# Attention scores of groups 3 to 7 from fp16 halves of the normalised input, in a cross-attention and feed-forward kernel

## What is computed

```python
Q = layernorm(x) @ Wq + bq;  K = ctx @ Wk + bk;  V = ctx @ Wv + bv
scores = where(mask, Q @ K.T / sqrt(512), -1e9)
x = x + softmax(scores) @ V @ Wo + bo
h = layernorm(x)
real = h @ cos(theta + theta_noise);  imag = h @ sin(phi + phi_noise)
out = x + sqrt(real**2 + imag**2)
```

## Time and profile before

| | us |
|---|---|
| median of 3 runs (244.76 to 245.19) | 244.77 |
| the profiled execution | 245.31 |
| its span | 243.20 |
| PE busy | 235.8 (97%) |
| DVE busy | 169.6 (70%) |
| ACT busy | 145.9 (60%) |
| POOL busy | 54.4 (22%) |

### The profile page before, as it was taken

One profiled execution on the slowest core, in us unless ns is written; L12 is line 12 of the kernel. 1 busy time (PEld: TensorE's weight loads), 2 busy tenths in 40 slices (PEclk: granted clock), 3 DMA queues, 4 the chain that ended last, 5 costly groups with the idle time before them and its releaser, 6 DMA issues.

```text
span 243.2 us, 3947 instructions
## 1 busy us (share of the span) xinstructions
PE 235.8 (97%) x1260; PEld 136.6 (56%) x1260; DVE 169.6 (70%) x341; ACT 145.9 (60%) x252; POOL 54.4 (22%) x154
## 2 busy tenths in 40 slices
PE   6999999999999999999999999999999999999993
PEld 2899437457544584458544854476447744444472
DVE  1676899976897876777768775877587753873443
ACT  2222787981669347943795379546873589266442
POOL 1002175410601233023302330132104310132000
PEclk9999999999999999999999999999999999999999
DMA  6999988695258724972397258734774324413622
GB/s 192 367 428 388 377 290 158 133 352 86 46 146 210 299 82 92 255 281 93 85 252 264 108 108 237 229 160 89 232 239 175 72 57 89 172 43 86 214 92 86
DMA packets 49533, 44.80 MB, mean 184 GB/s; under 512 B 42630, under 2 KB 42886, under 8 KB 46445
## 3 DMA queue, kind: packets, MB, share of 16 engines
q1 hardware_dynamic: 48565, 43.37, 57.7%
q0 software_dynamic: 288, 1.05, 2.4%
q10 hardware_dynamic: 664, 0.18, 0.3%
HBM read 25.66 MB, written 8.39 MB: 140 GB/s over the span
## 4 chain that ended last, share of the span: by engine, by line
PE 86%; DMA 7%; SPq 3%; ACT 2%; DVE 1%; issue 0%; DVEq 0%; ACTq 0%
PE re L503 9%; PE im L503 9%; PE im L504 9%; PE re L504 9%; PE re L505 9%; PE im L505 9%; PE score_bank L551 7%; DMA angle_n<-in_theta_noise 7%; PE att L481 3%; PE att L479 2%; PE re L564 2%; PE im L564 2%; PE re L566 2%; PE im L566 2%; PE re L568 2%; PE im L568 2%
## 5 line engine op out<-in xcount | busy, mean ns | idle before, releaser
L773 ACT ACTIVATE h<-x,shift,rstd 128x512 f32<-128x512 f32 x28 | 22.7, 811 | 34.6 <-POOL shift L382 34.6
L551 PEld LDWEIGHTS score_bank<-a_keys,xTb 128*128 128x128 f32 x192 | 35.9, 190 | 8.2
L503 PE MATMUL re<-w_hi,hT 128*128 128x512 f16 x100 | 37.9, 379 | 0.0
L503 PE MATMUL im<-w_hi,hT 128*128 128x512 f16 x100 | 37.9, 379 | 0.0
L505 PE MATMUL re<-w_hi,hT 128*128 128x512 f16 x100 | 37.9, 379 | 0.0
L505 PE MATMUL im<-w_hi,hT 128*128 128x512 f16 x100 | 37.9, 379 | 0.0
L504 PE MATMUL re<-w_lo,hT 128*128 128x512 f16 x100 | 37.9, 379 | 0.0
L504 PE MATMUL im<-w_lo,hT 128*128 128x512 f16 x100 | 37.9, 379 | 0.0
L1055 DVE SCALAR_TENSOR_TENSOR h_split<-h,h_split 128x512 f16<-128x512 f32 x32 | 22.1, 692 | 20.9 <-ACT h_split L777 20.2
L551 PE MATMUL score_bank<-a_keys,xTb 128*128 128x77 f32 x192 | 32.8, 252 | 0.0
L792 ACT ACTIVATE sq_re<-re 128x512 f32<-128x512 f32 x27 | 15.8, 586 | 17.2 <-PE re L505 12.1
(11 more groups left out here) (181 smaller groups left out, 425.7 us busy)
## 6 DMA issues: line engine op xcount, KB each, us to landing
xTb<-in_xT SPq DMA_DIRECT2D x8, 1024.0 KB, 5.2
xb<-in_x SPq DMA_DIRECT2D x7, 1024.0 KB, 5.5
out_rows<-wv SPq DMA_DIRECT2D x7, 1024.0 KB, 3.9
wk<-in_Wk SPq DMA_DIRECT2D x2, 512.0 KB, 5.5
wqT<-in_WqT SPq DMA_DIRECT2D x4, 256.0 KB, 7.8
wv<-in_Wv SPq DMA_DIRECT2D x1, 1024.0 KB, 13.6
wo<-in_Wo SPq DMA_DIRECT2D x1, 1024.0 KB, 16.1
xb<-in_x SPq DMA_DIRECT2D x4, 256.0 KB, 16.2
```

Of the source, the lines that this page charges most:

```text
L503: nc.tensor.matmul(bank_[:, :], hT[j][:, 0, k, :], w_hi[part][:, k, :], start=(k == 0), stop=False)
L551: last = nc.tensor.matmul(score_bank[:, KEYS * j:KEYS * j + KEYS], xTb[:, k, P * j:P * j + P], a_keys[:, k, KEYS * batch:KEYS * batch + KEYS],
L773: nc.scalar.activation(h[j % 2][:, :], x2[b][:, j, :], ACT.Identity, bias=shift2[:, j:j + 1], scale=rstd2[:, j:j + 1]).then_inc(h_made, 1)
```

## The change

Groups 3 to 7 no longer use `xTb`. Their scores are computed from the normalised x, `y`, in fp16 halves, as the feed products are. Per group: DVE takes the statistics (`stats_of_later_x`), POOL makes `y` in four fp32 tiles (in the place of `wo`, which is free by then), ACT makes the high half (`high_of_x`) and DVE the low half (`low_of_x`), SP turns both with a DMA transpose into `yT` (in the place of `angle_n`), four per group. `a_keys` is scaled by a norm and split once into `a_split`. A score is then two matmuls: the high half of y by both halves of the keys (154 columns) and the low half by the high half of the keys (77 columns, added to the first 77). The two halves of the sum lie side by side in `score_bank` and `pT_bank`, and `logits_of_halves` adds them in four operations. The load of x comes one step earlier, in three buffers in turn, and `load_xT` goes for these groups. On PE the scores move from `feed(n,2,1)` and `feed(n,3,0)` to `feed(n,3,0)` and `feed(n,3,1)`, the last two of the step.

```diff
 # POOL
+            def normal_of_x(m):
+                rstd_of_x(m)
+                pool.wait_ge(rstd1_made, m + 1)
+                if m > SPLIT:
+                    pool.wait_ge(y_lo_made, TILES * (m - SPLIT))
...
+                for j in range(TILES):
+                    nc.gpsimd.tensor_scalar(y[j], x_of[m][:, j, :], mv1[:, j, 0:1], rstd1[:, j:j + 1],
+                                            ALU.subtract, ALU.mult).then_inc(y_made, 1)
             def step(m):
-                rstd_of_x(m + 1)
+                if m < LAST:
+                    normal_of_x(m + 1)
                 for j in range(TILES):
                     rstd_of_x2(m, j)
 # PE
+            def score_halves(m, batch, i):
...
+                if k == 0:
+                    pe.wait_ge(yT_ready[j], 16 * (m - SPLIT + 1))
+                bank_ = (score_bank, pT_bank)[j // 2]
+                at = KK * (j % 2)
+                nc.tensor.matmul(bank_[:, at:at + KK], yT[j][:, 0, k, :], a_split[:, BATCH * k + batch, :, :],
+                                 start=(k == 0), stop=False)
+                last = nc.tensor.matmul(bank_[:, at:at + KEYS], yT[j][:, 1, k, :], a_split[:, BATCH * k + batch, 0, :],
+                                        start=False, stop=(k == CH - 1))
...
+            pe.wait_ge(a_squared, 1)
+            nc.tensor.matmul(pT_bank[:, 0:1], ones_all[:, :], a_part[:, :], start=True, stop=True).then_inc(a_norm_mm, 1)
 # ACT, step(n)
                 square(n, 0, 1)
+                if more:
+                    high_of_x(n + 2, 0)
                 roots(n - 1)
+                if more:
+                    high_of_x(n + 2, 1)
                 square(n, 1, 0)
+                if more:
+                    high_of_x(n + 2, 2)
+                    high_of_x(n + 2, 3)
 # DVE, step(n)
                     softmax_shift(m, a)
+                    if more:
+                        stats_of_later_x(n + 2)
                     low_probs(m)
                     softmax_total(m)
...
-                if blk is not None:
-                    stats_of_x(b, blk)
-                    dve.wait_ge(stats1_made, m + 2)
+                if more:
+                    low_of_x(n + 2, 0)
                 finish(n - 1, a)
+                if more:
+                    low_of_x(n + 2, 1)
                 residual(m, a, 0)
+                if more:
+                    low_of_x(n + 2, 2)
                 stats_of_x2(m, a, 0)
...
```

More of the change, by code:

```diff
@@ L61 @@
 V_SCALE = 8192.0
+A_SCALE = 8192.0
+SPLIT = 3
 WARM = 11
@@ L161, in build @@
         result = wv
+        x_of = [xb[0], xb[1], xb[0], wqT, xb[1], xb[0], wqT, xb[1]]
+        y = [wo[:, j, :] for j in range(TILES)]
+        y_halves = angle_n[0][:, :].bitcast(F16)
+        y_turned = angle_n[1][:, :].bitcast(F16)
+        y_split = [y_halves[:, 2 * DIM * j:2 * DIM * j + 2 * DIM].rearrange("p (s d) -> p s d", s=2) for j in range(TILES)]
+        yT = [y_turned[:, 2 * DIM * j:2 * DIM * j + 2 * DIM].rearrange("p (s c r) -> p s c r", s=2, c=CH) for j in range(TILES)]
+        a_squares = angle_w[0][:, 0:CH * KK]
+        a_pairs = a_keys[:, :, :].rearrange("p c (b k) -> p (c b) k", b=BATCH)
         re_bank = [bank("re0"), bank("re1")]
@@ L322, in _ @@
             transpose_h(1, [1])
-            with sp.Fori(0, 2) as i:
-                step(2 * i + 1, 1, i + 1, True)
-                step(2 * i + 2, 0, i + 2, True)
-            step(5, 1, 3, True)
-            step(6, 0, 4, False)
-            step(7, 1, 4, False)
+            load_later_x(SPLIT)
+            for n in range(1, GROUPS):
+                step(n)
             for j in range(TILES - 1):
@@ L599, in step @@
                 attend(n + 1, batch, 1)
[L600 to L603 removed]
+                feed(n, 2, 1)
                 attend(n + 1, batch, 2)
                 if more:
[L606 removed]
+                    feed_and_score(n, 3, 0, n + 2, 1 - batch, 0)
                 else:
@@ L609, in step @@
                 attend(n + 1, batch, 3)
-                feed(n, 3, 1)
+                if more:
+                    feed_and_score(n, 3, 1, n + 2, 1 - batch, 2 * CH)
+                else:
+                    feed(n, 3, 1)
             pe.wait_ge(a_ready, CH)
@@ L880, in step @@
                 high_half(n + 1, 1 - b, 2)
-            step(1, 1)
-            step(2, 0)
-            with act.Fori(0, 2) as i:
-                step(2 * i + 3, 1)
-                step(2 * i + 4, 0)
+            for n in range(1, LAST):
+                step(n, n % BATCH)
             square(LAST - 1, 3, 1)
@@ L1209, in step @@
                 mean_of_x2(m, 3)
-            step(1, 1, 1)
-            step(2, 0, 2)
-            step(3, 1, 2)
-            step(4, 0, 3)
-            step(5, 1, 3)
-            step(6, 0, None)
+            for n in range(1, LAST):
+                step(n, n % BATCH)
             add_squares(LAST - 1, 3)
```

155 lines of the change are left out of this document (120 added, 35 removed).

## The result

| | before | after |
|---|---|---|
| median, us | 244.76 (244.73 to 245.19, 4 runs) | 264.97 (264.71 to 265.8, 4 runs) |
| the profiled execution | 245.31 | 264.71 |
| its span | 243.20 | 262.9 |

The changed kernel takes 1.083 times as long, with a 95% interval of 1.080 to 1.085: 20.2 us more. The forecast was 257.1, with a range of 247 to 267; the narrower range that it gave its own mechanism, 254 to 261, doesn't hold the time.

The account below looks back on a forecast made before the run. TensorE bounds the kernel before; after the change an in-order chain of VectorE, ScalarE and GpSimd does. Step 1 +4.7, steps 2 to 5 +6.5, step 6 +1.1 give +12.3: 257.6 us profiled, 257.1 median, range 247 to 267.

Parts of the forecast that it names:

- The loop: In-order chain over VectorE, ScalarE and GpSimd, from root to root: 26.94 us a step against 25.32 before.
- Rival C: The loop holds, but GpSimd slips in before the low passes: 25.13 us a step, 247.5 us; chance 0.12.
- Rival D: GpSimd's pass takes 1.6 us or more and stops VectorE: 29 us a step, 267 us; chance 0.15.
- the forecast's own range: Range for the forecast's own mechanism, the loop: 254 to 261 us around 257.1; chance 0.53.
- GpSimd's first normalised tile 0.88: Link of the loop before ScalarE's high half; a 128x512 GpSimd pass priced 0.84, ends 0.62 and 1.6 us.
- the first root: ScalarE's root in step 1, put at 84.3, 2.72 us after GpSimd's first pass at 81.5.
- TensorE's pair: Two fp16 score matmuls replacing a 0.18 us fp32 one: 0.10 us, a gain of 1.25 us a step.
- the gain vanishes into idle time: TensorE's gain, 6.2 us over five steps, lost to new idle time before attend tile 2 and at step starts.
- The waits behind low pass 3 and low half 1: GpSimd's small operations wait for VectorE operations with two SBUF inputs: 0.80 and 0.69 us on the loop.
- Rival B: TensorE stays the limit, VectorE's and ScalarE's chain fitting 24.1 us a step: 239.6 us as median; chance 0.10.
- The queue on SP: Store behind the fourth transpose, next group's first transpose behind it: 0.6 us; 3.3 us from low half to landing.

Follow-up runs that it names:

- no_y_chain: Changed kernel without the normalised tiles of groups 3 to 7, their halves and transposes; scores take transposed h as weights: 243.6 us, ratio 0.990 to the kernel before.
- port_order: Changed kernel with VectorE's low pass 3 moved behind residual 1 and tile 0's low half behind residual 2: 262.4 us, ratio 1.066 to the kernel before.
- raw_halves_2: raw_halves with one change on SP's queue, tile 0's transpose sent ahead of the store: 240.8 us, ratio 0.983 to the kernel before.
- raw_halves: Changed kernel with halves of raw x, no y tiles, three 77-column matmuls per score and a new ScalarE and VectorE order: 244.2 us, 0.995 of the kernel before.
- root_first: Changed kernel with ScalarE's high half of normalised tile 0 moved behind the root: 263.8 us, ratio 1.072 to the kernel before.
- reordered: Changed kernel with all its work, in another order on ScalarE and VectorE, and the store ahead of the y transposes: 262.3 us, ratio 1.066 to the kernel before.

## Why the prediction was right, and where it was off

**The loop was right, station by station, up to GpSimd's first pass.** The range was wide enough for the time because it took in rivals C and D; the forecast's own range was missed by 4 us. Counted from the root at 142.09, the forecast's stations and the trace's:

| station | forecast | measured |
|---|---|---|
| GpSimd's second small operation of tile 0 (L428, 150.19) | 8.10 | 8.10 |
| low half of tile 0 through (next start, 153.44) | 11.41 | 11.35 |
| logits (159.70) | 17.64 | 17.61 |
| GpSimd's first pass gets in (168.36 less 2.07) | 24.22 | 24.20 |
| high half of x (168.36) | 25.10 | 26.27 |
| next root (170.30) | 26.94 | 28.21 |

**The step that failed** is "GpSimd's first normalised tile 0.88", with its bounds of 0.62 and 1.6: 2.07 measured. The forecast scaled a 128x128 operation (0.28) by columns and took an operation without length (0.10) as the fixed part. The pass's own slope is 3.3 ns a column for two arithmetic steps, with 0.36 fixed. The upper bound, two steps for twice the price, had the right idea and a slope that was too low. The pass makes 1.17 of the 1.27 by which a turn is longer; the other 0.10 lies between the high half and the root. The four turns make 5.1 us, and the first root, forecast for 84.3, starts at 85.66, of which the pass is 1.2. Together that is 6.5 of the 7.1 us by which the profiled execution, 264.71, exceeds the forecast's 257.6. The rest isn't assigned.

**TensorE's pair**: 0.10 forecast, 0.10 measured. The Trainium skill has 81 ns for load-and-matmul pairs of 128 columns ("TensorE: Matmul & The Clock Gate", Back-to-back issue gap); by the estimate from it the pair would take 0.16. That doesn't show here: the 77-column matmuls pass at 0.036 each between long ones. That the gain vanishes into idle time was right, and no_y_chain shows it is there to be had.

**The waits behind low pass 3 and low half 1** (0.80 and 0.69): the trace has 0.54 and 0.55 where 0.19 would do, at the two places that the forecast named. Rival C, without any such wait, is out. What both are worth together no run shows: port_order took the first away and got 0.71 a turn, with idle time of VectorE filled by the same edit.

**Rival D** had the pass above 1.6 and time and period nearly right (267, 29 a step), but by another mechanism: its passes reach into finish, and they do (4.57), yet VectorE isn't stopped by them in the changed kernel, and the fourth pass isn't on the loop. The time is the forecast's chain with a longer link. The Trainium skill's exclusive lock for a whole instruction, by either side ("SBUF — State Buffer", SBUF: two separate sides), agrees with the traces for GpSimd waiting on VectorE, and not for the other direction, which is shut until 0.62 of 2.07 us.

**Rival B** fell with the order and the waits, not with VectorE's amount of work: raw_halves_2 holds TensorE full beside the same 21 us of VectorE. With GpSimd's passes kept, no run does: the best has 25.6 a turn.

**The queue on SP** was priced at 0.6 us for the store behind four transposes, in 3.3 from low half to landing. That was too little: from the end of tile 0's low half to TensorE's first matmul are 3.93 us in the turn shown (153.44 to 157.37) and 5.8 in the first (97.02 to 102.79). It isn't on the loop, whose period follows the pass one to one. No run moves the store alone in the changed kernel. The two kernels that had the 1 MB store ahead of all four transposes paid for it: in raw_halves, sending the first transpose ahead of it gave 1.2% back.

## What to carry to other kernels

When no engine is full, write the turn of the loop as a chain of starts and price each link; work beside it is free, and a link costs one to one. Before moving an elementwise pass to GpSimd, measure that pass at its real length: a factor of 2.5 in one link was most of the error here. And ask of each new operand whether it needs what it waits for: the halves of the raw x needed no statistics, and that, with an order that starts them early, turned 20 us lost into 4 gained. And after a change of order look for the next wait: root_first, port_order and reordered each took one away and met another.
